# An eight-layer kernel: two LayerNorms placed in the stages before them, one mixture's turns placed two tiles ahead, value projections for two heads at a time

## What is computed

```python
x = x + L0_xattn(_layernorm(x), ctx)   # stage 0
x = x + L0_ffn(_layernorm(x))          # stage 1: 8 experts, 2 per token, and a shared expert
x = x + L1_xattn(_layernorm(x), ctx)   # stage 2: 16 heads of 128, "wide attention"
x = x + L1_ffn(_layernorm(x))          # stage 3: mixture of low-rank updates
x = x + L2_xattn(_layernorm(x), ctx)   # stage 4
x = x + L2_ffn(_layernorm(x))          # stage 5: 8 experts, 2 per token
x = x + L3_xattn(_layernorm(x), ctx)   # stage 6: attention over features
x = x + L3_ffn(_layernorm(x))          # stage 7: gated MLP and 8 of 512 small experts
```

```python
def _layernorm(x, eps=1e-05):
    m, v = mean(x), var(x)                       # over the 256 features
    return (x - m) / sqrt(v + eps)

def _L1_xattn_ref(inputs_q, inputs_kv, Wq, Wk, Wv, Wo):      # stage 2
    q = (inputs_q @ Wq).reshape(b, sq, 16, 128) * (1.0 / sqrt(128))
    k, v = inputs_kv @ Wk, inputs_kv @ Wv                    # per head
    attn = softmax(einsum('bqhd,bkhd->bhqk', q, k))
    return einsum('bhqk,bkhd->bqhd', attn, v).reshape(b, sq, 2048) @ Wo

def _L3_ffn_ref(h, W_q, keys, down_embed, up_embed, gate_w, up_w, down_w):   # stage 7
    scores2, idx2 = top_k((h @ W_q) . keys, 8)   # two halves, then 8 of the 64 sums
    ew = silu(h . down_embed[idx]) * softmax(scores)
    return silu(h @ gate_w) * (h @ up_w) @ down_w + ew . up_embed[idx]
```

## Time and profile before

| | us |
|---|---|
| median of 3 runs | 1188.53 |
| lowest, highest | 1183.68, 1190.47 |
| the profiled execution | 1184.68 |
| its span | 1182.9 |

### The profile page before, as it was taken

How to read it: one execution, slowest core, us unless ns; L and a number is a source line. 1 busy time by engine, 2 the same in 40 slices (tenths; PEclk the granted TensorE clock), 3 DMA queues, 4 the chain that set the end, 5 groups by cost and what they waited for, 6 DMA issues and landing times.

```text
span 1182.9 us, 18108 instructions
## 1 busy us (share of the span) xinstructions
PE 1048.6 (89%) x6946; PEld 707.2 (60%) x6946; DVE 573.4 (48%) x1312; ACT 369.3 (31%) x691; POOL 263.7 (22%) x340
## 2 busy tenths in 40 slices
PE   5877989979999999988874799999849999688989
PEld 4765578746676776767654577777613444343467
DVE  6976422245343534445566221212166778347792
ACT  3652123232212212112311121212104666536660
POOL 4221423330000000003331222222143344112350
PEclk9995999989999999989995999999957999979989
DMA  9002023211110100038008102111060000010000
GB/s 280 21 2 98 13 71 92 72 44 34 37 36 20 37 18 24 10 117 323 1 4 299 32 27 91 46 34 41 18 219 1 2 1 1 24 48 1 0 10 27
DMA packets 36427, 67.29 MB, mean 57 GB/s; under 512 B 4344, under 2 KB 26968, under 8 KB 34808
## 3 DMA queue, kind: packets, MB, share of 16 engines
q1 hardware_dynamic: 28952, 51.98, 12.9%
q0 software_dynamic: 4080, 11.15, 3.3%
q10 hardware_dynamic: 3312, 3.02, 0.7%
HBM read 54.72 MB, written 11.40 MB: 56 GB/s over the span
## 4 chain that ended last, share of the span: by engine, by line
PE 73%; DVE 16%; ACT 3%; issue 3%; DMA 3%; POOL 2%; SPq 0%; DVEq 0%; ACTq 0%
PE bank L347 19%; PE bank L1180 13%; PE bank L1204 7%; PE bank L1462 5%; PE bank L2148 4%; PE bank L2173 3%; PE bank L2194 3%; PE bank L1472 3%; PE bank L2588 3%; PE bank L1193 2%; PE bank L1447 2%; PE bank L1437 1%; PE bank L2212 1%; PE bank L2594 1%; DVE xs L274 1%
## 5 line engine op out<-in xcount | busy, mean ns | idle before, releaser
L1180 PE MATMUL bank<-big 128*128 x552 | 153.8, 422 | 3.6 <-ACT big L1054 2.4
L347 PE MATMUL bank<-XNT,big 128*128 128x512 f32 x296 | 139.9, 622 | 5.5 <-DVE big L2337 3.7
L1180 PEld LDWEIGHTS bank<-big 128*128 128x128 f32 x552 | 96.4, 191 | 50.5 <-issue 12.1
L268 POOL TENSOR_TENSOR rstd<-ve,half 128x1 f32<-128x1 f32 x64 | 38.8, 606 | 358.9 <-DVE ve L262 358.5
L2148 PE MATMUL bank<-big,xs 32*128 32x512 f32 x256 | 88.4, 738 | 19.1 <-DVE xs L274 18.1
L347 PEld LDWEIGHTS bank<-XNT,big 128*128 128x128 f32 x296 | 56.1, 197 | 71.1 <-issue 62.0
L2028 DVE TENSOR_REDUCE big<-bank 128x2 f32<-128x512 f32 x128 | 82.0, 685 | 24.5 <-PE bank L2148 23.9
L1204 PE MATMUL bank<-big 128*128 (+1 forms) x368 | 87.2, 380 | 1.1 <-ACT big L1069 1.1
L994 DVE TENSOR_TENSOR big<-big,bank 128x704 f32<-128x704 f32 x23 | 20.4, 889 | 124.7 <-ACT big L1062 124.7
L2100 ACT ACTIVATE big<-bank 128x1024 f32<-128x1024 f32 x64 | 64.9, 1025 | 38.7 <-PE bank L2173 38.4
L347 PE MATMUL bank<-CTXT,big 128*128 128x512 f32 (+1 forms) x192 | 67.0, 493 | 10.9 <-DMA big<-wvT 10.9
(11 more groups left out here) (346 smaller groups left out, 1810.3 us busy)
## 6 DMA issues: line engine op xcount, KB each, us to landing
big<-m_gu SPq DMA_DIRECT2D x8, 1408.0 KB
big<-a_qkv SPq DMA_DIRECT2D x16, 384.0 KB, 3.5
big<-m_d SPq DMA_DIRECT2D x8, 768.0 KB
yg<-big ACTq DMA_DIRECT2D x23, 128.0 KB, 2.1
big<-m_gu SPq DMA_DIRECT2D x8, 352.0 KB
big<-a_o SPq DMA_DIRECT2D x16, 128.0 KB, 2.1
xn<-XNT SPq DMA_DIRECT2D x8, 256.0 KB, 7.0
big<-f_keys SPq DMA_DIRECT2D x1, 2048.0 KB, 9.3
```

The source lines that it names most:

```text
L268: e.tensor_tensor(k.rstd[p][:, :], k.ve[p][:, :], k.half[:, :], ALU.pow).then_inc(k.ln_rstd, 1)
L347: ins = e.matmul(out, a, b, start=start and n == 0, stop=stop and n == len(pairs) - 1)
L1180: ins = e.matmul(out, xgT[s % 2][:, kb, :], WB[:, bass.ds(at[s] + (kb * 2 * F + c * chunk), chunk)], start=kb == 0, stop=kb == KB - 1)
```

## The change

- **Buffers.** `mv`, `ve` and `rstd` have one column or pair for each of the 8 tiles.
- **Stage 2's LayerNorm in stage 1.** Behind each tile's two adds DVE takes this tile's statistics. Normalising of tiles 0 and 1 stands behind tile 5, of 2 and 3 behind tile 6, of 4 to 7 behind tile 7. POOL takes the power of four tiles in one instruction, ahead of the gathers for tile 7, and then of three and of one. PE turns tiles 0 to 3 inside its last value projection of `pe_first`, 4 to 7 behind it; ACT copies two tiles at a time.
- **Stage 7's LayerNorm in stage 6.** DVE takes statistics and normalises behind units 28 to 31; PE turns tiles 0 to 3 before the last unit's values, 4 and 5 before the last sort; `pe_first` of stage 7 runs `gate_up` 0, turn 6, query half 0, `gate_up` 1, turn 7, query half 1.
- **Stage 1's turns.** Turns 0 and 1 stand inside `shared_down`, later ones two slots ahead; the one wait for all of `shy` becomes one for each bank.
- **Values in stage 2.** The first four heads' values are one product of 128x512 per tile; later ones are computed for two heads at a time, four tiles in each of two consecutive heads, with moving operands of 256 columns. The weights are loaded apart (`a2_qk`, `a2_vf`, `a2_v`).

```diff
@@ experts, pool
+            if t == NT - 1 and k.front.get(2):
+                k.front[2]["rstd"](e, 0, 4)
@@ experts, dve, behind the adds of tile t
+            if shared_expert and k.front.get(2):
+                k.front[2]["stats"](e, t)
+                for n in {5: (0, 1), 6: (2, 3), 7: (4, 5, 6, 7)}.get(t, ()):
+                    k.front[2]["norm"](e, n)
@@ experts, act
         rows(0)
+        if LAG:
+            rows(1)
...
-            if s + 1 < TILES and LAG:
-                rows(s + 1)
+            if s + 2 < TILES and LAG:
+                rows(s + 2)
@@ experts, pe
-            after(e, "inv", 1)
-            for t in range(NT):
-                shared_down(t)
-            after(e, "shy", NT)
...
             if s >= 1 + LAG:
                 after(e, "h_sb", s - LAG)
+            elif shared_expert:
+                after(e, "shy", NT - 1 + s)
...
+        if shared_expert:
+            after(e, "inv", 1)
+            for t in range(NT):
+                shared_down(t)
+                if t >= NT - 3 and t < NT - 1:
+                    turn(t - (NT - 3))
...
-            if s + 1 < TILES:
-                turn(s + 1)
+            if s + 1 + LAG < TILES:
+                turn(s + 1 + LAG)
@@ attention_wide
+    def value_steps(h):
+        if not FIRST - 1 <= h < H - 1:
+            return None
+        n = h - (FIRST - 1)
+        return n // 2, n % 2, n
@@ attention_wide, sp
+        e.wait_ge(S["f_ps"], 2 * FIRST)
+        load_v(0)
+        load_v(1)
         for h in range(H):
             if h + FIRST < H:
-                if h < FIRST:
-                    e.wait_ge(S["qk_ps"], qk_at(h + 1))
-                else:
-                    e.wait_ge(S["v_ps"], h - FIRST + 1)
+                e.wait_ge(S["qk_ps"], qk_at(h + 1))
                 load(h + FIRST)
...
+            if h % 2 == 0 and 4 <= h < H - FIRST:
+                e.wait_ge(S["v_ps"], h - 2)
+                load_v(h // 2)
@@ attention_wide, pe
+        def values(pair, half, n):
+            e.wait_ge(vsem[pair % 2], vsem_at[pair % 2] + 16 * (pair // 2 + 1))
+            if n > 0:
+                e.wait_ge(S["v_sb"], n)
+            for i in range(4):
+                t = 4 * half + i
+                ins = mm(e, bank[:, VB + i // 2, (i % 2) * 2 * HD:(i % 2 + 1) * 2 * HD],
+                         [(k.CTXT[:, kb, t * P:(t + 1) * P], wv[pair % 2][:, kb]) for kb in range(KB)])
+            ins.then_inc(S["v_ps"], 1)
@@ feature_attention, act
         front = k.front.get(7)
+        if front:
+            front["rows"](e, 0)
+            front["rows"](e, 2)
         sums(NT - 1)
+        if front:
+            front["rows"](e, 4)
         sorted_out(NT - 1)
@@ feature_attention, pe
+        if front:
+            for t in range(4):
+                front["turn"](e, t)
         values(NU - 1, 0)
         values(NU - 1, 1)
+        if front:
+            for t in (4, 5):
+                front["turn"](e, t)
         sort(NT - 1)
@@ peer_mlp
+                          dve_behind={(2, 0): (("stats", (0, 1)),), (2, 1): (("stats", (2, 3)),),
+                                      (3, 0): (("stats", (4, 5)), ("norm", (0, 1))), (3, 1): (("norm", (2, 3)),),
+                                      (5, 1): (("norm", (4, 5)), ("stats", (6,)), ("norm", (6,)))})
...
+    def act_first(e):
+        front_rows(e, 6, 1)
...
-        for t in range(4):
-            turned(t)
         silu(0)
-        for t in range(4, NT):
-            turned(t)
+        front_rows(e, 7, 1)
...
+    def pe_first(e):
+        e.wait_ge(S["ld"], 16 * 6)
+        e.wait_ge(k.xt_sb, at0 + 4 + CREDIT)
+        gate_up(e, 0)
+        front_turn(e, 6)
+        e.wait_ge(k.f6_out, k.f6_out_at)
+        project(e, 0)
+        gate_up(e, 1)
+        front_turn(e, 7)
+        project(e, 1)
```

More of the change, by code:

```diff
@@ L154, in shared @@
     k.st = [k.sb(f"st{p}", [P, 6]) for p in (0, 1)]
-    k.mv = [k.sb(f"mv{p}", [P, 2]) for p in (0, 1)]
-    k.ve = [k.sb(f"ve{p}", [P, 1]) for p in (0, 1)]
-    k.rstd = [k.sb(f"rstd{p}", [P, 1]) for p in (0, 1)]
+    k.mv = [k.sb(f"mv{t}", [P, 2]) for t in range(NT)]
+    k.ve_all, k.rstd_all = k.sb("ve", [P, NT]), k.sb("rstd", [P, NT])
+    k.ve = [k.ve_all[:, t:t + 1] for t in range(NT)]
+    k.rstd = [k.rstd_all[:, t:t + 1] for t in range(NT)]
+    k.front = {}
     k.ident = k.sb("ident", [P, P])
@@ L1206, in down @@
             tell(ins, "y_ps")
+        if shared_expert:
[4 more added lines that the diff above has]
+                    turn(t - (NT - 3))
+        after(e, "wts", ends["wts"])
+        after(e, "eid", 1)
         place(0)
-        turn(0)
+        if not shared_expert:
+            turn(0)
         for s in range(TILES + 1 + LAG):
@@ L1238, in attention_wide @@
     W, W2 = Arena(k.late, 2048), Arena(k.late[:, 6900:8800], 1900)
-    w3 = [a.take(3, KB, HD) for a in (W, W, W2, W2)]
+    wqk = [a.take(2, KB, HD) for a in (W, W, W, W2)]
+    wv_first = W2.take(KB, FIRST * HD)
+    wv = [wv_first[:, n].rearrange("p (c f) -> p c f", c=KB) for n in (0, 1)]
     wo = [W.take(D) for _ in (0, 1)]
@@ L1249, in attention_wide @@
     kT = [A.take(T) for _ in range(FIRST)]
-    v = [A.take(NT, HD) for _ in range(FIRST)]
+    v = A.take(FIRST, NT, HD)
     S = {n: k.sem("a2_" + n) for n in
@@ L2013, in dve @@
         ch = k.chain(e, "dve")
+        front = k.front.get(7)
         def norm(t):
@@ L2054, in rest @@
                 quotient(t - 1) if half == 0 else final(t - 1)
+            if front:
+                for f, tiles in front["dve_behind"].get((u - LAST, half), ()):
+                    for t in tiles:
+                        front[f](e, t)
         e.wait_ge(k.masks, masks0 + 2)
@@ L2074, in dve @@
         final(NT - 1)
+        if front:
+            front["stats"](e, NT - 1)
+            front["norm"](e, NT - 1)
     def act(e):
@@ L2288, in peer_mlp, with front_stats, front_norm, front_turn @@
     TURN, QB, WT, OUT = 4, 6, 4, 6
+    XS = k.big[:, 0:2048].rearrange("p (t d) -> p t d", d=D)
+    DONE6 = LOADED + 8 * l
+    def front_stats(e, t):
+        e.wait_ge(k.x_tile, DONE6 - NT + t + 1)
+        ln_stats_dve(e, k, k.chain(e, "dve"), t, t % 2)
+    def front_norm(e, t):
+        e.wait_ge(k.ln_rstd, at0 + t + 1)
+        e.tensor_scalar(XS[:, t], k.X[:, t, :], k.mv[t][:, 0:1], k.rstd[t][:, 0:1], ALU.subtract, ALU.mult)\
+            .then_inc(k.ln_out, 1)
+    def front_turn(e, t):
+        e.wait_ge(k.ln_out, at0 + t + 1)
+        e.wait_ge(k.xt_sb, at0 + CREDIT + (7 if t == 7 else max(t // 2 * 2 - 2, 0)))
+        for kb in range(KB):
+            ins = e.transpose(k.bank[:, TURN + t // 2 % 2, t % 2 * D + kb * P:t % 2 * D + (kb + 1) * P],
+                              XS[:, t, kb * P:(kb + 1) * P], k.ident[:, :])
+        ins.then_inc(k.xt_ps, 1)
+    def front_rows(e, t, n=2):
+        e.wait_ge(k.xt_ps, at0 + t + n + CREDIT)
+        dst = k.XNT[:, :, t // 2 * 2 * P:(t // 2 + 1) * 2 * P].rearrange("p k (h q x) -> p k h q x", h=2, q=2)
+        for q in range(t % 2, t % 2 + n):
+            src = k.bank[:, TURN + t // 2 % 2, q * D:(q + 1) * D].rearrange("p (k x h) -> p k h x", k=KB, h=2)
+            e.copy(dst[:, :, :, q], src).then_inc(k.xt_sb, 1)
+    if l >= 6:
+        k.front[7] = dict(stats=front_stats, norm=front_norm, turn=front_turn, rows=front_rows,
+                          dve_behind={(2, 0): (("stats", (0, 1)),), (2, 1): (("stats", (2, 3)),),
+                                      (3, 0): (("stats", (4, 5)), ("norm", (0, 1))), (3, 1): (("norm", (2, 3)),),
+                                      (5, 1): (("norm", (4, 5)), ("stats", (6,)), ("norm", (6,)))})
     def rows(j, h):
@@ L2307, in sp, with pool_first @@
         e.wait_ge(S["st"], 16 * NT)
+    def pool_first(e):
+        if l >= 6:
+            for t in range(NT):
+                ln_rstd_pool(e, k, at0 + t, t % 2)
     def pool(e):
-        for t in range(NT):
-            ln_rstd_pool(e, k, at0 + t, t % 2)
+        for t in (1,):
             if t == 1:
@@ L2615, in pe @@
             ins.then_inc(S["k_ps"], 1)
-        for n in range(1, IB):
-            gate_up(n)
+        for n in range(2, IB):
+            gate_up(e, n)
         for n in range(EB):
@@ L2620, in pe @@
         for n in range(IB):
-            gate_up(IB + n)
+            gate_up(e, IB + n)
             if n % 2 == 1:
```

216 lines of the change are left out of this document (111 added, 105 removed).

## The result

The changed kernel takes 1148.76 us (1144.83 to 1149.69, 4 runs) against 1188.86 (1183.68 to 1190.47, 4 runs) of the kernel before: ratio 0.9664, interval 0.9626 to 0.9701. Measured once more later, it took 1150.46 us (5 runs) against 1184.06 (9 runs), ratio 0.9706 (0.9678 to 0.9733). So it is faster by 34 to 40 us.

A forecast was written before the change was run, and what follows sets the result against it. PE (89% busy, chain of waits mostly through it) was taken as the bound, idling chiefly at two LayerNorms and stage 1's loop start. Savings 3.1 + 6.5 + 2.7 + 11.9 = 24.2 from 1188.5 gave 1164.3 us, range 1157 to 1171.5.

The forecast's parts named there:

- Part 1: Stage 1's turns done ahead: first slots 1.8 us shorter, `gate_up` 0 starting 1.2 us earlier; sum given as 3.1 us.
- its 20 full slots only shift: Rest of stage 1 after the loop's start: slots keep their length and merely move earlier, no gain counted.
- Part 2: Stage 2's LayerNorm hidden behind stage 1's last gathers: first projection at 252.1 instead of 258.64, 6.5 us saved.
- rival (a): Clock stays up at both resumed places, before stage 2 and in stage 7: 1.7 + 1.0 us more, 1161.6; chance 0.13.
- a pause of 3.3 us: PE's pause before stage 2's first projection, down from 10.9 us; clock still expected to fall, as after a 3.86 us wait.
- Part 3: Stage 2's values for two heads at a time: twelve steps save 0.21 us each, plus a 0.2 wait; 2.7 us.
- Part 4: Stage 7's LayerNorm inside stage 6's tail: scores 10.1 us earlier, DVE waits 2.8 less, clock 1.0 off; 11.9 us.
- the 1.0 taken off for the clock: Stage 7, before `embed` 0: PE's wait grows to about 4.2 us and slows what follows; 1.0 us lost (0 to 1.9).
- the row at 1082.99: Earlier trace row in stage 7; by it alone no clock loss, and that LayerNorm's gain would be 12.9 us.
- Rival (b): Stage 7 gives part back through longer PE waits, fallen clock or returning DVE waits: gain 7 to 8, 1168.5; chance 0.17.
- (c): Stage 2's LayerNorm yields only 1 to 2 us, DVE behind the gathers, POOL's power holding the last: 1169.5; chance 0.07.
- (d): Slower than before: stage 2's value weights land late and PE stands waiting; 1189 us or more; chance 0.03.

The follow-up runs named there:

- c1_pause_2us: Changed kernel with four more DVE instructions between tile 7's statistics and the last four normalisings before stage 2; `scores` 0 came 4.0 and 3.3 us later.

## Why the slot became shorter

Inside `gate_up` stands the load of the next expert's place into a register of PE's sequencer. Two pieces of the timeline, the first of the kernel before, the second of the changed one (PEld is the weight load; the edge of the asked window cuts the first row):

```profile
189.47 1.41 PE L1180 MATMUL bank<-big 128*128 x6
190.31 0.45 PEld L1180 LDWEIGHTS bank<-big 128*128 128x128 f32 x3 [0.35 <-issue]
```

```profile
179.03 1.30 PEld L1192 LDWEIGHTS bank<-big 128*128 128x128 f32 x8
179.24 1.36 PE L1192 MATMUL bank<-big 128*128 x8
```

Before, the weight loads stop for 0.35 us in the middle, and nothing that the profile shows is waited for; after, all eight run through. The profile gives the load itself a duration of 0.30 us, and 46 of them in either kernel.

The profile also dates the loads. The first row below is the one inside `gate_up` 3 of the kernel before, the second the one inside `gate_up` 4 of the changed kernel (durations in ns, then the start in us):

```profile
L1171 PEldq TENSOR_LOAD <-big x1: 298/298/298, 161.4 to 161.4; - x1
L1181 PEldq TENSOR_LOAD <-big x1: 314/314/314, 154.9 to 154.9; - x1
```

Before, the load starts at 161.4, when the matmuls of its own `gate_up` have just begun (161.32). After, it starts at 154.9, and its `gate_up` begins at 156.76: the sequencer is 1.9 us ahead of the array and has done with the load before the array gets there.

The Trainium skill, in "Perfetto Trace Analysis", section "Sequencer Loop", has the sequencer push engine instructions into a queue and carry out control instructions itself. By that rule a load costs nothing while the queue is filled ahead of it, and the two rows agree. What held the sequencer back is read from the program: at its head `gate_up` waits for the copy of the tile turned last, and before the change this copy ended at 163.88 us for the `gate_up` that begins at 164.12:

```profile
163.51 0.37 ACT L1054 COPY big<-bank 128x256 f32<-128x256 f32 x1
```

Three kernels put numbers on the load.

```diff
                 if c == 0 and s + 1 < TILES:
-                    place(s + 1)
+                    at[s + 1] = at[s]
```

> The kernel before, in which stage 1's loop reads the expert's place into PE's register once ahead of slot 0 and never again (it leaves out the choice of the expert: all slots of stage 1 use the first one's weights). Theory (the register load inside gate_up stands bare, because PE's sequencer waits for the copy of the tile just turned and so has nothing queued ahead): the slot falls from 2.80 to about 2.53 us with the turns still only one tile ahead, 5 to 6 us earlier at the last product. Rival (the shorter slot of the changed kernel comes from the data's way, the turned rows being there earlier, and not from the load): the slot stays at 2.80.

With a second `place(s + 1)` behind the first, in the kernel before and in the changed one:

> The kernel before with the same register load done twice in each slot of stage 1. Theory: the second load is as bare as the first and takes 0.3 us of load and some 0.3 us of register instructions behind it, so the slot grows from 2.80 to 3.3 to 3.45 us. Rival (the load is hidden behind matmuls): it stays at 2.80.

> The changed kernel with the same register load done twice in each slot of stage 1. Theory: the sequencer runs most of a slot ahead of the array, so the second load is hidden as the first is: the slot stays at 2.50 us, at most 2.6. Rival (the load costs the same in both kernels and the 0.30 came from elsewhere): it grows by 0.5 to 0.65 to about 3.1.

Their slots, PE, in this order:

```profile
176.66 1.36 PE L1180 MATMUL bank<-big 128*128 x8
179.16 1.36 PE L1180 MATMUL bank<-big 128*128 x8
```

```profile
178.54 0.76 PE L1180 MATMUL bank<-big 128*128 x4
179.98 0.86 PE L1180 MATMUL bank<-big 128*128 x4 [0.68 <-issue]
181.98 0.76 PE L1180 MATMUL bank<-big 128*128 x4
```

```profile
175.60 1.43 PE L1192 MATMUL bank<-big 128*128 x8
178.16 1.39 PE L1192 MATMUL bank<-big 128*128 x8
180.69 1.60 PE L1192 MATMUL bank<-big 128*128 x8
```

Without the load the kernel before has slots of 2.50 us, with the turns still one tile ahead, and its last product comes 5.8 us earlier relative to the tri matmul. With two loads it has 3.44, all of the second load bare. The changed kernel carries two in about 2.6 (2.56 and 2.53 here, 0.09 above 2.50 on average from `gate_up` 3 on). One load: 0.30 bare or nothing; two: 0.94 bare or 0.1. Only while the loop fills is the second load partly bare in the changed kernel too: `gate_up` 3 comes 38.4 us behind the tri matmul in place of 36.8. So what the load costs is shown, and that it depends on where the turns stand.

## The granted clock

Much of what moves in the table's unchanged stretches is the clock. In the last stage PE waits 2.63 to 2.66 us for a `turn_w` in every kernel. Behind it, in the first profile of the kernel before, and in its second:

```profile
1131.30 0.66 PE L2578 MATMUL bank<-ident,big 128*128 128x128 f32 x4 [2.64 <-DVE big L2392]
1135.55 5.49 PE L2588 MATMUL bank<-big 128*128 128x256 f32 x16 [0.69 <-ACT big L2472]
```

```profile
1131.00 0.66 PE L2578 MATMUL bank<-ident,big 128*128 128x128 f32 x4 [2.64 <-DVE big L2392]
1134.06 3.72 PE L2588 MATMUL bank<-big 128*128 128x256 f32 x16 [0.69 <-ACT big L2472]
```

The same wait in the same code, and from 1128 to 1142 us the mean granted clock is 0.76 in the first and 1.00 in the second; over all the profiles it fell behind this wait in 2 of 16. The matmuls near 15 us differ in the same way (2.07 or 1.16 us for eight; here only the durations speak, since the granted clock reads 1.00 in either case). In all 16 profiles the short form goes with a tri matmul at 117.3 to 117.6 us (5 of them) and the long one with 119.2 to 119.9 (11), which is the 2 us in the table's first row. The Trainium skill, in "TensorE: Matmul & The Clock Gate", part 1, calls the number of slow matmuls of one kernel variable from run to run; the traces agree.

The 4.6 us in stages 3 to 6 are the clock only in part. The last `out_proj` of stage 2, with which the stretch begins, takes 4.01 us in one profile of the changed kernel and 5.38 in the other. But 1.1 us are a longer wait at the start of stage 6 (18.52 and 19.64 us, PE for the first normalised tile, behind gathered rows), and the rest is spread in steps of under 0.6 us that were not traced one by one; the mean granted clock of the stretch is 0.92 and 0.91.

In front of stage 2 it looks otherwise. Extra DVE instructions between the statistics of tile 7 and the last normalisings lengthen the pause:

```diff
+                if t == NT - 1:
+                    for _ in range(8):
+                        ch.step(e.tensor_scalar(k.xs[0][:, :], k.X[:, 0, :], 1.0, None, ALU.mult))
```

> The changed kernel with eight more DVE instructions, one behind the other (about 4 us), between the statistics of tile 7 and the last four normalisings in front of stage 2. The wait ahead of the first projection grows by as much. Theory (the clock stayed up in the changed kernel because the pause is short and has the transposes in it; behind a longer one it falls, as in the kernel before): the first projection's 8 instructions take 5.3 us in place of 3.67, so it costs 4 + 1.7 = 5.7 us. Rival (the clock stays up here for another reason, the work ahead of the pause): 3.67 us and 4 us in all.

> The changed kernel with four more DVE instructions (1.3 us by the eight that took 2.62) between the statistics of tile 7 and the last four normalisings in front of stage 2. PE's idle time ahead of the transposes grows from 0.75 to some 2.1 us, where it was 3.87 with eight. Theory (the clock falls only behind a stretch in which PE does nothing for long, and its transposes count against it): the clock stays up, first projection 3.67 us, cost 1.3 us. Rival (any longer pause is enough): 5.3 to 6.1 us and 3.5 us or more in all.

> The same kernel as c1_pause_2us. If the clock's fall at the first projection is set by the length of the wait ahead of it, it falls again (8 instructions in about 6.3 us). If it is a matter of phase, as at the wait of 2.64 us in the last stage, behind which the clock fell in the kernel before and not in the changed one, it may stay up (3.67 us).

> The changed kernel with two more DVE instructions (0.65 us) at the same place: PE's wait ahead of the transposes becomes about 1.4 us. It was 0.75 to 1.13 where the clock stayed up and 1.76 and 3.87 where it fell. Threshold between: either. If it stays up, the delay costs 0.65 us, if it falls 3.4.

The eight instructions took 2.6 us, less than I expected, and `scores` 0 came 6.0 us later behind the tri matmul than in the first profile of the changed kernel (130.7 against 124.7 us), so this theory holds. The second profile of the changed kernel, the one with two instructions, and the one with eight:

```profile
237.95 1.41 PE L1350 MATMUL bank<-ident,big 128*128 128x128 f32 x8 [1.22 <-DVE big L1342]
240.13 3.67 PE L354 MATMUL bank<-XNT,big 128*128 128x512 f32 x8 [0.78 <-ACT XNT L1356]
```

```profile
238.49 1.41 PE L1353 MATMUL bank<-ident,big 128*128 128x128 f32 x8 [1.68 <-DVE big L1345]
240.67 5.10 PE L354 MATMUL bank<-XNT,big 128*128 128x512 f32 x8 [0.78 <-ACT XNT L1359]
```

```profile
241.36 1.76 PE L1353 MATMUL bank<-ident,big 128*128 128x128 f32 x8 [3.87 <-DVE big L1345]
243.89 6.05 PE L354 MATMUL bank<-XNT,big 128*128 128x512 f32 x8 [0.78 <-ACT XNT L1359]
```

With four the wait was 1.76 us in one execution and 2.41 in the other, and the projection took 6.74 and 5.27; `scores` 0 came 4.0 and 3.3 us later than in the first profile of the changed kernel. So at this place the clock stayed up with waits of 0.24 to 1.22 us ahead of the transposes (five profiles) and fell with 1.68 to 3.87 (four). It goes with the length of the wait here, and the theory that the clock stays up with four instructions was wrong: 0.5 us more than the second profile of the changed kernel has costs 1.4 us and above on top of itself. How the clock comes to fall behind 1.68 us here, and mostly not behind 2.64 us in the last stage, is open.

> The kernel before once more. Theory: places at which the code is the same differ between its two profiles as they do between the two of the changed kernel: the tri matmul of stage 1 at 119.6 or 2 us earlier, the first down product of the last stage at 5.5 or 3.7 us. The slot of stage 1 stays at 2.80 us, and scores 0 follows the tri matmul by 145.0 us.

As expected: slots of 2.80, 145.0 us from the tri matmul to `scores` 0, and 2.3 us less at the tri matmul and 1.8 less at the down product.

## A version that goes further

> The changed kernel with three more moves. (1) In stage 5's loop the turn of the next tile stands ahead of the down product and no longer behind it, so that its copy is there before gate_up asks for it and PE's sequencer can run ahead of the array over the register load. Theory: the slot of stage 5 falls from 8.35 to 8.19 us (0.10 of it bare load inside gate_up, 0.06 ahead of it), 24 slots, 3.9 us. Rival (what stands bare there is not the load): the slot stays at 8.35. (2) At the start of the last stage gate_up 1 is cut: three of its four products stand around the turn of tile 7 and one behind the second half of the queries, so the keys' scores begin about 1.6 us earlier. (3) In front of stage 2 tiles 4 and 5 are normalised behind tile 6: 0.2 us. In all 5.7 us less than the changed kernel, ratio to the kernel before about 0.962.

> The changed kernel once more, on the chip and in the rounds of the others, as their base. Ratio to the kernel before 0.966. Its profile shows what of the profiled 39.8 us was the clock's phase in stage 0: the tri matmul stood at 117.45 us in its first profile and at 119.5 to 119.9 in four kernels out of seven profiled since. If that is phase alone and not the change, it may stand at either place here.

```diff
+            if s + 1 + LAG < TILES and not LAG:
+                turn(s + 1)
             if not LAG and s >= 1:
                 down(s - 1)
-            if s + 1 + LAG < TILES:
+            if s + 1 + LAG < TILES and LAG:
                 turn(s + 1 + LAG)
```

Measured 1143.36 us, ratio to before 0.9650 (0.9628 to 0.9671), against 1150.46 and 0.9706 of the changed kernel timed with it: 7 us less where 5.7 were expected. Both expected ratios were missed (0.962 here, 0.966 for the changed kernel, whose interval of 0.9678 to 0.9733 leaves it out): against 1184.06 us the changed kernel gains 33.6 us, against the 1188.86 of the first measurement it gained 40.1. Stage 5, in the second profile of the changed kernel and in this one:

```profile
704.56 5.00 PE L1192 MATMUL bank<-big 128*128 x16
712.91 3.52 PE L1192 MATMUL bank<-big 128*128 x11
```

```profile
692.83 4.90 PE L1192 MATMUL bank<-big 128*128 x16
701.03 4.90 PE L1192 MATMUL bank<-big 128*128 x16
```

The slot falls from 8.35 to 8.20 us, and the 0.10 inside `gate_up` is gone. The load inside it starts at 704.7 in the first piece, behind the start of the matmuls (704.56), and at 699.9 in the second, 1.1 us ahead of them (701.03): the theory of the bare load holds in a stage that the change had not touched. The stage has 23 slots, not the 24 of my expectation: 3.4 us. The keys' scores follow the sort by 12.67 us, 1.58 less. The third move shows nothing: the stretch to `scores` 0 is 37.12 us, between the changed kernel's two. Some 2 of the 7 us have no place of their own; they are of the size by which the clock moves a run.

## Why the prediction was wrong in size

- **Part 1, the start.** Forecast 3.1, measured 4.9 to 5.1. The register load was left in front of `gate_up` 0 with 0.8 us, and the fill was costed with slots of 2.80. Both are the same error as the next: the first load now starts at 146.5 us, while PE is still at the shared product, and `gate_up` 0 comes 2.1 us earlier and not 1.2; the three slots behind it take 5.5 us and not 6.5. (The recorded terms, 1.8 and 1.2, make 3.0 and not 3.1.)
- **Part 1, "its 20 full slots only shift".** This is the step that failed: the term was put at nothing, and it measured 6.3 us. The 19 distances from `gate_up` 3 to the last one fell from 2.82 us on average to 2.50, the last of them to 2.28. I had split a slot into `gate_up` 1.50, turns and down product and had taken the sum for PE's work. The earlier trace rows shows 1.66 to 1.83 for eight instructions whose later form needs 1.36, and one bare load is in it. I read a duration as work, in the loop where the change lets a wait of the sequencer be met earlier. With the start this is some 8 of the 9.4 to 13.5 us that the forecast lacks.
- **Part 2.** The mechanism was as worked out, the power of four columns 0.15 us shorter than taken, the last gather the limit: the last tile's adds start 3.67 us behind those of the tile before, where the pair before has 2.88. The clock was the miss: rival (a) was right here, 1.7 us. I had compared a pause of 3.3 us with the wait of 3.86 in the earlier trace rows; but the pause holds eight transposes, and the waits inside it were 0.75 and 0.78. With a wait of 3.87 at this place, in the experiment above, the clock does fall: the row was read rightly and laid beside the wrong thing.
- **Part 3.** 2.7 as forecast; the form gained 0.12 a step instead of 0.21, and a clock that fell less at the loop's end (1.0 us) made up for it. A right sum from a wrong term, by luck.
- **Part 4.** 10.0 us to the keys' scores as forecast (10.1), and the two DVE waits of 2.8 went, nearly all in the second profile (29.39 us from the keys' scores to `embed` 0 against 32.04) and half in the first (30.64), where the clock fell at the keys. The wait before `embed` 0 did not grow, so the 1.0 taken off for the clock was wrong, and the row at 1082.99 right. Rival (b) did not come. Another 0.3 to 2.6 us behind `embed` 0 are the clock in the kernel before.
- **Slower, or not doing what it says:** rivals (c) and (d) did not come. DVE still waits 1.04 us for the last gather, and from the fourth head of the loop to the fifteenth each follows the one before by 18.51 or 18.52 us, without a wait for the value weights.
- **The range** took in the bounds of the terms, and no term for something in a loop that I had declared unchanged. It ignored as well that one profile may lie several us off another of the same kernel (5.6 between the two of the changed kernel). The 40.1 us of the first measurement hold some 6 us that the later one does not have; that part of the miss is the difference between executions, not a step of the sum.

## What to carry to other kernels

When an edit lets a wait at the head of a loop's slot be met earlier, look at what the sequencer does behind that wait, register loads above all, and compare the duration of the repeated group with the same group where nothing is bare; the difference times the number of trips is at stake. Loads of registers belong behind enough queued work. Profile a kernel twice before a microsecond of a granted-clock effect is charged to an edit.

## What the runs showed of the hardware

A register load takes PE's sequencer 0.30 us (slots of 2.80 and 2.50 us with and without it), and a second one, bare and with what follows it, adds 0.64 us (3.44). Where the sequencer is 1.9 us ahead of the array one load costs nothing and two cost 0.09 a slot. The power on GpSimd took 0.66, 0.92 and 1.05 us for 1, 3 and 4 columns. In one profile the gathered rows of one tile came 1.9 us late (4.47 us behind the tile before, against 2.54 in the changed kernel). In front of stage 2 the clock fell in four of four profiles with waits of 1.68 to 3.87 us and in none of five with 0.24 to 1.22.
